# Two cross steps to one output copy, and transposes moved into the middle of the self steps, in a decoder layer's attention

## The chip, the cores and the metric

The kernel runs on one core of a Trainium2 chip. The metric is the device time of one execution in microseconds (us), as the median of several runs. TensorE (PE) does the matrix products and writes them to eight banks of PSUM; VectorE (DVE) and ScalarE (ACT) read the banks; GpSimd (POOL) works in SBUF alone; PEld is TensorE's weight load.

## The reference, cut to what matters

For eight batches of 512 tokens with 256 features the reference does a first attention, then a second attention of 16 heads of 16 features, over the 512 tokens themselves (causal) and over a context of 1024 tokens, then a routed feed-forward part, each followed by a layer norm. The change touches the second attention alone:

```python
o_self  = softmax(causal(q_s @ k_s.T * scale)) @ v_s     # 16 heads, 512 x 512
o_cross = softmax(q_c @ k_c.T * scale) @ v_c             # 16 heads, 512 x 1024
x = layernorm(x + (o_self + o_cross) @ Wp + bp)
```

Everything in it is in fp32.

## The kernel before, in words

The 16 heads are four groups of four. A group's four heads lie in four row groups of 32 rows of TensorE, and four products of one step run side by side. The loop over `s` in `batch` has 48 steps: 16 self steps (four key tiles for each of four groups, of 512, 384, 256 and 128 query columns) and 32 cross steps (eight key tiles for each group, always 512 columns). A step makes three kinds of products.

- `scores(m, r)` makes the scores of a query tile by keys. VectorE takes the maximum of each row (`maxima`, L1131 for self, L1134 for cross). These run ahead: while step `s` is worked on, the maxima of `m = s + 7` and later are taken. There are four of them (r = 0 to 3) in a cross step, and four or eight in a self step (steps 3, 7, 11 and 15 have eight).
- `scoresT(s, g)` makes the same scores transposed (L1669 for self, L1672 for cross). ScalarE takes their exponential into `work` (`probabilities`, L751), four in a step.
- `pv_part(p)` multiplies the exponentials by the values (`weighted_values`, L1681) into one bank. ScalarE copies the bank to `featA` or `featB` (`part_out`, L759), and GpSimd adds it to `featA` (`add_part`, L607). Up to step 35 one such part stands for every step; from step 36 on the products of four steps gather in one bank without such copies.

Two further products are transposes: `max_rows` turns a group's maxima (L1635), which VectorE then adds to the queries (`put_rows`, L1160) before that group's first step; `o_transpose` turns a group's outputs (L1719), which VectorE then divides by the sums (`finish`, L1168, L1170 and for cross L1174).

An fp32 product runs through TensorE in two passes, and each pass is a row of the trace. The four row groups are filled by `scores` and `scoresT` in turn, so a step of 512 columns shows as four waves of four matmuls, first the two passes of r = 0, 1 and g = 0, 1, then those of r = 2, 3 and g = 2, 3. `weighted_values` fills four column groups instead, in two waves.

Who may write a bank is settled by two rings, both walked in an order written down beforehand. Banks 0 to 3 are VectorE's ring: the scores for the maxima, the transposed rows and outputs take them in turn (`slot_uses`), and `free_slot` makes TensorE wait until VectorE is done with the use four places before. Banks 4 to 7 are ScalarE's ring: the four transposed scores of a step and its part take them in turn (`exp_slot_uses`), and `free_exp_slot` makes TensorE wait for ScalarE in the same way. From step 37 on the banks are shared out differently. TensorE takes its instructions strictly in the order in which they are written, so a product whose bank isn't free holds up all behind it.

```python
def free_exp_slot(use):
    if use >= EXP_RING:
        what, n = exp_order[use - EXP_RING]
        if what == "exp":
            pe.wait_ge(pT_ready, b * ALL_SCORES + n + 1)
        else:
            pe.wait_ge(part_copied, b * PARTS + n + 1)
```

Of the kernel before, what the change touches and what calls it, by code (L numbers as in the profile page):

```python
# [37 lines left out]
def decoder_layer(nc, x, xT, ctxT, conv_w, pe_w, qkT, vT, outT, Wk, bk, Wq, bq, Wv, bv, Wck, bck, Wcq, bcq,  # L38
# [40 lines left out]
    RING, EXP_RING = 4, 4  # L79
    BURST = 4  # L80
    BURSTS = STEPS // BURST
    PART = 1
    CHUNKS = 16
    EXTRAS = NT + 2
    EXTRA_BANKS = (7, 6, 0, 5, 7, 1)
# [16 lines left out]
    PARTS = EARLY_STEPS // PART  # L102
# [16 lines left out]
    with ctx:  # L119
# [182 lines left out]
        def spare_row(i):  # L302

            return HD * (1 - i % 2)
# [26 lines left out]

        def parts_behind(s):

            ends = [(p, PART * (p + 1) - 1) for p in range(PARTS)]
            return [p for p, e in ends if s == e + (2 if e < SELF_STEPS else 1)]

        def opens_rows(p):

            return part_of(PART * p)[2] == 0

        def adds_before(p):

# [3 lines left out]

        def part_columns(p):

            kind, _, u = part_of(PART * p)
            return slice(P * u if kind == SELF else 0, S)  # L350

        def o_rows(kind, i):
# [2 lines left out]

        def part_rows(p):

            kind, i, _ = part_of(PART * p)
            return (o_rows(kind, i) if opens_rows(p) else featB[:, adds_before(p) % 2, :])[:, part_columns(p)]

        def last_part(kind, i):

            return (first_step(kind, i) + (NT if kind == SELF else NC)) // PART - 1

        def outputs_ready(s):

# [3 lines left out]
        def slot_uses(ffn):  # L370

            order = []

            def take_maxima(first, end):
                for m in range(first, end):
                    order.extend(("max", m, g) for g in range(GH))

            for m in range(LEAD):
                if m == NT + 2:
                    order.append(("rows", SELF, 0))  # L380
                take_maxima(m, m + 1)
                if ffn and m == EXPERT_LEAD:
                    order.append(("expert",))
            for s in range(ALL_STEPS):
                if s == LATE_STEP:
                    late = len(order)
                take_maxima(maxima_before(s), maxima_before(s + 1))
                order.extend(("pv", j) for j in outputs_ready(s) if j >= SINGLES_FROM)
                order.extend(("rows",) + part for part in rows_behind(s))
                order.extend(("o",) + part for part in outputs_behind(s))  # L390
# [121 lines left out]
        def _(pool):  # L512
# [75 lines left out]
            def batch(b, prev=True, ahead=2):  # L588
# [9 lines left out]
                def add_part(p):  # L598

                    pool.wait_ge(part_copied, b * PARTS + p + 1)  # L600
                    own_wait(nc.gpsimd)
                    if adds_before(p):
                        pool.wait_ge(part_added, b * ADDS + adds_before(p))
                        own_wait(nc.gpsimd)
                    kind, i, _ = part_of(PART * p)
# [39 lines left out]
        def _(act):  # L645
# [37 lines left out]
            def batch(b, prev=True, ahead=True):  # L683
# [152 lines left out]
        def _(dve):  # L836
# [206 lines left out]
            def batch(b, prev=True, ahead=2):  # L1043
# [76 lines left out]

                def maxima(m):

                    kind, i, u = part_of(m)
                    for r in range(GH):
                        use, g = uses["max", m, r], (r + 2) % GH
                        dve.wait_ge(slot_in, base + use + 1)
                        scores = slot(uses, use)
                        if kind == SELF:
                            n = P * (u + 1)
                            own_wait(nc.vector)  # L1130
                            nc.vector.tensor_tensor_reduce(masked[:, g, 0:n], scores[:, 0:n], mask_w[:, S - n:S], -1.0, -MASKED, ALU.add, ALU.min,  # L1131
                                                           top_s[:, i % 2, u, GW * g + spare_row(i):GW * g + spare_row(i) + 1]).then_inc(slot_out, 1)
                        else:
                            nc.vector.tensor_reduce(top_half[:, i % 2, g, u // 2, u % 2:u % 2 + 1], scores, AX.X, ALU.max,  # L1134
                                                    negate=True).then_inc(slot_out, 1)
                    if kind == CROSS and u == NC - 1:
# [51 lines left out]
                for s in range(ALL_STEPS):  # L1188
# [10 lines left out]
                    for m in range(maxima_before(s), maxima_before(s + 1)):  # L1199
                        maxima(m)  # L1200
# [3 lines left out]
                    for part in rows_behind(s):  # L1204
# [3 lines left out]
                    for part in outputs_behind(s):  # L1208
                        finish(*part)
                if ahead:  # L1210
                    scores1(b + 1, 0)
# [89 lines left out]
        def _(pe):  # L1301
# [113 lines left out]
            def batch(b, prev=True, ahead=True):  # L1415
# [333 lines left out]
                for s in range(ALL_STEPS):  # L1749
                    first, n = maxima_before(s), maxima_before(s + 1) - maxima_before(s)  # L1750
                    for g in range(GH):
                        for r in range(n * g, n * (g + 1)):
                            scores(first + r // GH, r % GH)
                        scoresT(s, g)
                        if g == GH - 1 and s - SINGLES_BEHIND >= BURST * SINGLES_FROM:
# [3 lines left out]
                    for part in rows_behind(s):  # L1759
                        max_rows(*part)  # L1760
                    for part in outputs_behind(s):
                        o_transpose(*part)
                pv_step(ALL_STEPS - 2)
                if ahead:
# [84 lines left out]
```

## Time and profile before

| what | value |
|---|---|
| median of 3 runs | 2258.28 us (2256.73 to 2265.44) |
| the profiled execution's own time | 2258.12 us |
| its span, first to last instruction | 2256.4 us |
| mean granted TensorE clock | 0.964 of full speed |
| busy share PE, DVE, ACT, POOL | 94%, 81%, 66%, 23% |
| the 16 self steps of batch 2 (697.3 to 753.7 us) | 56.4 us |
| its cross steps 16 to 35 (753.7 to 816.4 us) | 62.7 us |
| its cross steps 36 to 47 (816.4 to 844.7 us) | 28.3 us |

The span holds eight batches, one after the other, each with a first attention and projections and then the 48 steps. A step is told by the start of its first exponential on ScalarE; batch 2 is taken as the example throughout. Busy time on PE covers waits inside a pipelined row of matmuls, so that it is the starts of the waves that tell the pace.

### The profile page before, as it was taken

How to read it: one execution, taken by the hardware profiler on the slowest of the kernel's cores; microseconds unless marked ns; L12 is line 12 of the kernel's file. 1: busy time of each engine (PE TensorE's matmuls, PEld its weight loads, DVE VectorE, ACT ScalarE, POOL GpSimd, SP SyncE). 2: the span in 40 equal slices, each digit the busy share in tenths (PEclk: the TensorE clock that was granted, in tenths of full speed). 3: DMA queues.
4: the chain of work that ended last, by engine and by line, in shares of the span. 5: the costliest groups of instructions: out<-in, count | busy, mean ns of one | idle time of the engine just before them, and what ended most of it. 6: DMA issues, size and time to landing. Idle time of an engine off the chain costs nothing.

```text
span 2256.4 us, 39042 instructions
## 1 busy us (share of the span) xinstructions
PE 2129.1 (94%) x13092; PEld 930.7 (41%) x13138; DVE 1835.3 (81%) x5029; ACT 1495.0 (66%) x3265; POOL 519.1 (23%) x641
## 2 busy tenths in 40 slices
PE   5999999999999999999999999999999999989983
PEld 2344334543345434444335433454334543345332
DVE  6857869689887889778897888968888788978864
ACT  2935887458864688457894588745886468845761
POOL 3012330133211350123401233013321132002310
PEclk7899999999999999999999999999999999999995
DMA  3700025000430006100170002500043000510000
GB/s 109 136 10 1 1 58 92 11 1 1 94 66 10 2 12 120 29 11 1 29 131 10 1 1 63 97 10 1 1 85 66 11 1 11 111 30 2 1 10 10
DMA packets 250857, 81.79 MB, mean 36 GB/s; under 512 B 236065, under 2 KB 247329, under 8 KB 250657
## 3 DMA queue, kind: packets, MB, share of 16 engines
q1 hardware_dynamic: 250656, 79.29, 17.3%
q8 instruction: 105, 1.72, 0.3%
q14 instruction: 96, 0.78, 0.1%
HBM read 16.35 MB, written 4.19 MB: 9 GB/s over the span
## 4 chain that ended last, share of the span: by engine, by line
PE 72%; DVE 14%; ACT 9%; issue 4%; DMA 1%; SPq 0%; POOL 0%; DVEq 0%; POOLq 0%; ACTq 0%
PE bank L1622 15%; PE bank L1681 13%; PE bank L1672 9%; PE bank L1308 6%; ACT work L692 6%; PE bank L1618 5%; PE bank L1669 4%; PE bank L1575 4%; DVE work L871 3%; PE bank L1438 3%; PE bank L1425 2%; PE bank L1461 2%; DVE top_half L1134 2%; PE bank L1635 1%; PE bank L1719 1%
## 5 line engine op out<-in xcount | busy, mean ns | idle before, releaser
L751 ACT ACTIVATE work<-bank 128x512 f32<-128x512 f32 (+3 forms) x1536 | 725.3, 550 | 329.9 <-PE bank L1669 203.0
L1134 DVE TENSOR_REDUCE top_half<-bank 128x1 f32<-128x512 f32 x1024 | 633.7, 681 | 84.4 <-PE bank L1622 83.5
L1622 PE MATMUL bank<-k_c,q_c 32*128 32x512 f32 x2048 | 559.9, 630 | 0.0
L1672 PE MATMUL bank<-q_c,k_c 32*128 32x512 f32 x2048 | 463.3, 627 | 3.9 <-DVE top_half L1134 3.9
L692 ACT ACTIVATE work<-work,neg 128x512 bf16<-128x512 bf16 x512 | 362.6, 715 | 30.5 <-DVE work L871 29.8
L1681 PE MATMUL bank<-work,v_flat 128*32 128x512 f32 (+3 forms) x3072 | 368.9, 556 | 3.1 <-DVE featA L1153 1.8
L871 DVE TENSOR_SCALAR_CACHE_REDUCE work<-bank 128x512 bf16<-128x512 f32 x512 | 322.2, 685 | 41.1 <-PE bank L1407 31.6
L607 POOL TENSOR_TENSOR featA<-featA,featB 128x512 f32<-128x512 f32 (+3 forms) x232 | 241.9, 1043 | 374.2 <-ACT featB L759 374.1
L1131 DVE CUSTOM_DVE_ANT_0 masked<-bank,mask_w 128x384 bf16<-128x384 f32 (+3 forms) x512 | 225.3, 488 | 100.3 <-PE bank L1618 96.1
L1622 PEld LDWEIGHTS bank<-k_c,q_c 32*128 32x128 f32 x2048 | 228.8, 186 | 163.5 <-DVE top_half L1134 113.5
L1669 PE MATMUL bank<-q_s,k_s 32*128 32x512 f32 (+3 forms) x1024 | 240.0, 477 | 0.0
L1672 PEld LDWEIGHTS bank<-q_c,k_c 32*128 32x128 f32 x2048 | 179.5, 184 | 107.6 <-ACT work L751 66.9
L595 POOL TENSOR_SCALAR_AFFINE_SELECT work<-work 128x512 f32<-128x512 f32 x128 | 81.2, 635 | 549.6 <-ACT work L751 549.6
L1618 PE MATMUL bank<-k_s,q_s 32*128 32x384 f32 (+3 forms) x1024 | 194.7, 474 | 4.6 <-DVE top_s L1131 4.4
L568 POOL TENSOR_SCALAR ln_var<-mv 128x4 f32<-128x4 f32 x32 | 8.8, 275 | 752.5 <-DVE mv L880 752.5
L1681 PEld LDWEIGHTS bank<-work,v_flat 128*32 128x32 f32 x3072 | 62.1, 108 | 280.6 <-ACT work L751 267.6
L1425 PE MATMUL bank<-k,q 32*128 32x512 bf16 x448 | 139.8, 389 | 16.4 <-DVE work L871 14.5
L1669 PEld LDWEIGHTS bank<-q_s,k_s 32*128 32x128 f32 x1024 | 136.5, 188 | 35.1 <-issue 25.1
L759 ACT COPY featB<-bank 128x512 f32<-128x512 f32 (+3 forms) x232 | 121.2, 522 | 24.7 <-PE bank L1681 24.6
L1438 PE MATMUL bank<-work,v 128*32 128x512 bf16 x512 | 134.6, 389 | 0.9 <-DMA work<-work 0.8
L1618 PEld LDWEIGHTS bank<-k_s,q_s 32*128 32x128 f32 x1024 | 97.7, 186 | 78.9 <-DVE top_s L1131 35.1
L1064 DVE TENSOR_SCALAR work<-work,rden 128x512 bf16<-128x512 bf16 x424 | 123.0, 349 | 4.5
(200 smaller groups left out, 2434.3 us busy)
## 6 DMA issues: line engine op xcount, KB each, us to landing
xT_pad<-xT SPq DMA_DIRECT2D x16, 256.0 KB, 2.9
ctx_sb<-ctxT SPq DMA_DIRECT2D x8, 512.0 KB, 3.4
x_res<-x SPq DMA_DIRECT2D x8, 512.0 KB, 5.0
out<-r_sb SPq DMA_DIRECT2D x8, 512.0 KB, 2.9
work<-work SPq DMA_TRANSPOSE x112, 4.4
qk_sb<-qkT SPq DMA_DIRECT2D x1, 512.0 KB, 5.1
pe_sb<-pe_w SPq DMA_DIRECT2D x1, 256.0 KB, 4.1
v_sb<-vT SPq DMA_DIRECT2D x1, 256.0 KB, 5.7
```

The source lines that it names most:

```text
L607: nc.gpsimd.tensor_tensor(rows, rows, part_rows(p), ALU.add).then_inc(part_added, 1)
L692: nc.scalar.activation(e1[:, h % E1_SLOTS, t, :], s1[:, h % 2, t, :], ACT.Exp, bias=neg1[:, h % 2, t:t + 1], scale=-1.0, accum_out=den1[:, ...
L751: nc.scalar.activation(pT[:, s % PT_SLOTS, g, q0:S], exp_bank(n)[:, 0:S - q0], ACT.Exp, scale=SCALE).then_inc(pT_ready, 1)
L871: nc.vector.tensor_scalar(s1[:, h % 2, t, :], bank[:, (NT * h + t) % A1_BANKS, :], -SCALE, None, ALU.mult, ALU.min, accum_out=neg1[:, h % ...
L1131: nc.vector.tensor_tensor_reduce(masked[:, g, 0:n], scores[:, 0:n], mask_w[:, S - n:S], -1.0, -MASKED, ALU.add, ALU.min, top_s[:, i % 2, u ...
L1134: nc.vector.tensor_reduce(top_half[:, i % 2, g, u // 2, u % 2:u % 2 + 1], scores, AX.X, ALU.max, negate=True).then_inc(slot_out, 1)
L1438: last = mm(bank[GW * g:GW * (g + 1), PV1_BANKS[h // 8], :], v1[:, h, j, :], p1T[:, h % E1_SLOTS, :, j, :], start=(h % 2 == 0 and j == 0), ...
L1618: mm(dst[:, 0:n], q_s[rows, i, P * u:n], k_s[rows, i, 0:n], start=True, stop=True, tile_position=(GW * g, 0)).then_inc(slot_in, 1)
L1622: mm(dst, q_c[rows, i, P * t:P * (t + 1)], k_c[rows, i, S * half:S * (half + 1)], start=True, stop=True, tile_position=(GW * g, 0)).then_i ...
L1669: mm(dst[:, 0:S - q0], k_s[rows, i, q0:q0 + P], q_s[rows, i, q0:S], start=True, stop=True, tile_position=(GW * g, 0)).then_inc(sT_mm, 1)
L1672: mm(dst, k_c[rows, i, P * u:P * (u + 1)], q_c[rows, i, :], start=True, stop=True, tile_position=(GW * g, 0)).then_inc(sT_mm, 1)
L1681: last = mm(dst[GW * g:GW * (g + 1), q0:S], v_flat[:, at:at + GW], pT[:, s % PT_SLOTS, g, q0:S], start=start, stop=stop, tile_position=(0, ...
```

## The change

The list `PART_STEPS` takes the place of the constant `PART = 1`. The 16 self steps keep one part each; cross steps 16 to 35 make one part for two steps, ten parts where there were twenty. Such a part multiplies the exponentials of two steps by their values into one bank, behind the step that follows the second of the two (step 18, 20, ... 36), and ScalarE copies and GpSimd adds it once. A batch has 26 parts where it had 36.

Second, in the self steps the transposes of the next group's rows (steps 2, 6, 10) and of a group's outputs (steps 7, 11, 15) no longer stand behind the step's products. They stand between its second and third quarter, on TensorE between `scoresT` of g = 1 and g = 2, on VectorE between the two halves of the step's maxima, and in VectorE's ring at that place. The rows of the first cross group (step 14) and all transposes of cross steps stay where they were.

```diff
-    PART = 1
+    PART_STEPS = [range(s, s + 1) for s in range(SELF_STEPS)] + [range(s, s + 2) for s in range(SELF_STEPS, EARLY_STEPS, 2)]
+    PARTS = len(PART_STEPS)
...
-            ends = [(p, PART * (p + 1) - 1) for p in range(PARTS)]
+            ends = [(p, steps[-1]) for p, steps in enumerate(PART_STEPS)]
             return [p for p, e in ends if s == e + (2 if e < SELF_STEPS else 1)]
+        def part_with(s):
+            return next(p for p, steps in enumerate(PART_STEPS) if s in steps)
...
+        def middle_rows(s):
+            return [part for part in rows_behind(s) if s < SELF_STEPS and part != (CROSS, 0)]
+        def middle_outputs(s):
+            return outputs_behind(s) if s < SELF_STEPS else []
+        def maxima_tiles(s):
+            tiles = [(m, r) for m in range(maxima_before(s), maxima_before(s + 1)) for r in range(GH)]
+            return tiles[:len(tiles) // 2], tiles[len(tiles) // 2:]
...
-                take_maxima(maxima_before(s), maxima_before(s + 1))
+                ahead_tiles, behind_tiles = maxima_tiles(s)
+                order.extend(("max",) + tile for tile in ahead_tiles)
+                order.extend(("rows",) + part for part in middle_rows(s))
+                order.extend(("o",) + part for part in middle_outputs(s))
+                order.extend(("max",) + tile for tile in behind_tiles)
...
-                            act.wait_ge(part_mm, b * PARTS + (s - PT_SLOTS) // PART + 1)
+                            act.wait_ge(part_mm, b * PARTS + part_with(s - PT_SLOTS) + 1)
...
-                    first, end = PART * p, PART * (p + 1)
+                    first, end = PART_STEPS[p][0], PART_STEPS[p][-1] + 1
                     free_exp_slot(exp_uses["part", p])
...
                         scoresT(s, g)
+                        if g == GH // 2 - 1:
+                            for part in middle_rows(s):
+                                max_rows(*part)
+                            for part in middle_outputs(s):
+                                o_transpose(*part)
```

On TensorE, cross steps 24 to 26 stand so before the change: each is eight products (scores L1622 and transposed scores L1672 in turn), and the values of the step before (L1681, four heads) follow it. The rows are the end of step 24 and the start of step 25.

```order
305 L1622 MATMUL bank<-k_c,q_c 128x512
306 L1672 MATMUL bank<-q_c,k_c 128x512
307 L1681 MATMUL bank<-work,v_flat 32x512 x4
308 L1622 MATMUL bank<-k_c,q_c 128x512
309 L1672 MATMUL bank<-q_c,k_c 128x512
```

After the change the same place reads so (scores L1662, transposed scores L1712, values L1721): the end of step 24, the values of steps 22 and 23, and the eight products of step 25, behind which step 26 begins at once.

```order
301 L1662 MATMUL bank<-k_c,q_c 128x512
302 L1712 MATMUL bank<-q_c,k_c 128x512
303 L1721 MATMUL bank<-work,v_flat 32x512 x8
304 L1662 MATMUL bank<-k_c,q_c 128x512
305 L1712 MATMUL bank<-q_c,k_c 128x512
```

Four value products in each gap between two steps have become eight in every other gap, and none in the gaps between.

On ScalarE the copies of the parts (L759 before, L788 now) stand between the exponentials (L751 before, L780 now); before the change, these are the copies of steps 25, 26 and 27, with the exponentials of steps 27 and 28 between them.

```order
107 L759 COPY featB<-bank 128x512
108 L751 ACTIVATE work<-bank 128x512 x4
109 L759 COPY featB<-bank 128x512
110 L751 ACTIVATE work<-bank 128x512 x4
111 L759 COPY featB<-bank 128x512
```

In the changed kernel these are the copies of steps 24 with 25, 26 with 27, and 28 with 29.

```order
98 L788 COPY featA<-bank 128x512
99 L780 ACTIVATE work<-bank 128x512 x8
100 L788 COPY featB<-bank 128x512
101 L780 ACTIVATE work<-bank 128x512 x8
102 L788 COPY featB<-bank 128x512
```

Eight exponentials stand between two copies where four stood.

The third place is self step 10 on TensorE, with the transposes of the last self group's rows. Before the change, from the third quarter of the step to the start of the next:

```order
171 L1669 MATMUL bank<-q_s,k_s 128x256
172 L1622 MATMUL bank<-k_c,q_c 128x512
173 L1669 MATMUL bank<-q_s,k_s 128x256
174 L1681 MATMUL bank<-work,v_flat 32x512 x4
175 L1635 MATMUL bank<-ident,top_s 128x128 x4
176 L1622 MATMUL bank<-k_c,q_c 128x512 x2
```

And after it:

```order
169 L1709 MATMUL bank<-q_s,k_s 128x256
170 L1675 MATMUL bank<-ident,top_s 128x128 x4
171 L1662 MATMUL bank<-k_c,q_c 128x512
172 L1709 MATMUL bank<-q_s,k_s 128x256
173 L1662 MATMUL bank<-k_c,q_c 128x512
174 L1709 MATMUL bank<-q_s,k_s 128x256
175 L1721 MATMUL bank<-work,v_flat 32x512 x4
176 L1662 MATMUL bank<-k_c,q_c 128x512 x2
```

The four transposes have moved from behind the values to ahead of the second half of the step's products.

## Rows read from the trace of the kernel before

**Rows 1.** The page, its first two parts: busy engines, and the granted clock.

```profile
PE 2129.1 (94%) x13092; PEld 930.7 (41%) x13138; DVE 1835.3 (81%) x5029; ACT 1495.0 (66%) x3265; POOL 519.1 (23%) x641
...
PEclk7899999999999999999999999999999999999995
```

**Rows 2.** The page's chain of work that ended last, by engine.

```profile
PE 72%; DVE 14%; ACT 9%; issue 4%; DMA 1%; SPq 0%; POOL 0%; DVEq 0%; POOLq 0%; ACTq 0%
```

**Rows 3.** Windows of batch 2: length, busy PE, PEld, DVE, ACT, POOL, clock.

```profile
697.30:753.70 56.40, 56.26 (x433) 28.54 (x431) 48.29 (x126) 29.80 (x79) 17.42 (x26) 1.00 0.02 8
753.70:816.40 62.70, 62.70 (x512) 24.30 (x508) 54.76 (x92) 51.13 (x102) 21.00 (x19) 1.00 0.00 1
```

**Rows 4.** Groups by line, cross steps 16 to 35: busy, mean ns | idle before, releaser.

```profile
L1134 DVE TENSOR_REDUCE top_half<-bank 128x1 f32<-128x512 f32 x80 | 49.6, 682 | 8.0 <-PE bank L1622 8.0
L751 ACT ACTIVATE work<-bank 128x512 f32<-128x512 f32 x81 | 42.0, 603 | 12.1 <-PE bank L1672 12.1
...
L1622 PEld LDWEIGHTS bank<-k_c,q_c 32*128 32x128 f32 x160 | 17.1, 183 | 14.7 <-DVE top_half L1134 11.1 <-issue 2.5
```

**Rows 5.** Timeline of PE, cross steps 25 and 26: start us, us, instruction.

```profile
780.23 0.69 PE L1622 MATMUL bank<-k_c,q_c 32*128 32x512 f32 x1
...
781.62 0.59 PE L1672 MATMUL bank<-q_c,k_c 32*128 32x512 f32 x1
...
782.16 1.06 PE L1681 MATMUL bank<-work,v_flat 128*32 128x512 f32 x8
783.15 0.69 PE L1622 MATMUL bank<-k_c,q_c 32*128 32x512 f32 x1
...
783.68 0.59 PE L1622 MATMUL bank<-k_c,q_c 32*128 32x512 f32 x1
...
784.12 0.59 PE L1622 MATMUL bank<-k_c,q_c 32*128 32x512 f32 x1
...
785.13 1.07 PE L1681 MATMUL bank<-work,v_flat 128*32 128x512 f32 x8
786.13 0.69 PE L1622 MATMUL bank<-k_c,q_c 32*128 32x512 f32 x1
```

**Rows 6.** Timeline of DVE, cross steps 25 and 26.

```profile
781.38 2.48 DVE L1134 TENSOR_REDUCE top_half<-bank 128x1 f32<-128x512 f32 x4 [0.49 <-PE bank L1622]
784.31 2.48 DVE L1134 TENSOR_REDUCE top_half<-bank 128x1 f32<-128x512 f32 x4 [0.45 <-PE bank L1622]
```

**Rows 7.** Timeline of ACT, the same steps.

```profile
784.41 2.06 ACT L751 ACTIVATE work<-bank 128x512 f32<-128x512 f32 x4 [0.38 <-PE bank L1672]
786.34 0.62 ACT L759 COPY featB<-bank 128x512 f32<-128x512 f32 x1
```

**Rows 8.** Timeline of DVE, self steps 10 and 11.

```profile
731.44 0.69 DVE L1160 TENSOR_TENSOR q_s<-bank,q_s 128x512 f32<-128x512 f32 x1 [0.20 <-PE bank L1635]
732.49 4.87 DVE L1134 TENSOR_REDUCE top_half<-bank 128x1 f32<-128x512 f32 x8 [0.36 <-PE bank L1622]
737.56 0.26 DVE L1168 RECIPROCAL rec<-bank 128x16 f32<-128x16 f32 x1 [0.20 <-PE bank L1719]
```

**Rows 9.** Timeline of PE, end of self step 10 and start of step 11.

```profile
729.75 1.07 PE L1681 MATMUL bank<-work,v_flat 128*32 128x512 f32 x8
730.75 0.66 PE L1635 MATMUL bank<-ident,top_s 128*128 128x128 f32 x4
731.33 0.70 PE L1622 MATMUL bank<-k_c,q_c 32*128 32x512 f32 x2
```

**Rows 10.** Timeline of PEld at 732.1 us, behind the rows' addition.

```profile
732.18 0.29 PEld L1622 LDWEIGHTS bank<-k_c,q_c 32*128 32x128 f32 x2 [0.32 <-DVE q_s L1160]
```

**Rows 11.** Windows: self step 7 at either clock, batch 2 and batch 3.

```profile
717.70:723.80 6.10, 6.10 (x40) 2.98 (x42) 5.54 (x15) 1.63 (x6) 1.58 (x2) 1.00 0.00 1
985.10:993.90 8.80, 8.80 (x40) 3.69 (x41) 5.74 (x16) 1.83 (x6) 1.63 (x2) 0.65 0.01 2
```

More of the change, by code:

```diff
@@ L347, in part_columns @@
         def part_columns(p):
-            kind, _, u = part_of(PART * p)
+            kind, _, u = part_of(PART_STEPS[p][0])
             return slice(P * u if kind == SELF else 0, S)
@@ L356, in part_rows, with end_rows, end_outputs @@
         def part_rows(p):
-            kind, i, _ = part_of(PART * p)
+            kind, i, _ = part_of(PART_STEPS[p][0])
             return (o_rows(kind, i) if opens_rows(p) else featB[:, adds_before(p) % 2, :])[:, part_columns(p)]
         def last_part(kind, i):
-            return (first_step(kind, i) + (NT if kind == SELF else NC)) // PART - 1
+            return part_with(first_step(kind, i) + (NT if kind == SELF else NC) - 1)
+        def middle_rows(s):
+            return [part for part in rows_behind(s) if s < SELF_STEPS and part != (CROSS, 0)]
+        def end_rows(s):
+            return [part for part in rows_behind(s) if part not in middle_rows(s)]
+        def middle_outputs(s):
+            return outputs_behind(s) if s < SELF_STEPS else []
+        def end_outputs(s):
+            return outputs_behind(s) if s >= SELF_STEPS else []
+        def maxima_tiles(s):
+            tiles = [(m, r) for m in range(maxima_before(s), maxima_before(s + 1)) for r in range(GH)]
+            return tiles[:len(tiles) // 2], tiles[len(tiles) // 2:]
         def outputs_ready(s):
@@ L386, in slot_uses @@
                     late = len(order)
-                take_maxima(maxima_before(s), maxima_before(s + 1))
+                ahead_tiles, behind_tiles = maxima_tiles(s)
[3 more added lines that the diff above has]
+                order.extend(("max",) + tile for tile in behind_tiles)
                 order.extend(("pv", j) for j in outputs_ready(s) if j >= SINGLES_FROM)
-                order.extend(("rows",) + part for part in rows_behind(s))
-                order.extend(("o",) + part for part in outputs_behind(s))
+                order.extend(("rows",) + part for part in end_rows(s))
+                order.extend(("o",) + part for part in end_outputs(s))
             order += [("pv", ALL_STEPS // BURST - 1), ("o", CROSS, HG - 1)]
@@ L604, in add_part @@
                         own_wait(nc.gpsimd)
[L605 removed]
+                    kind, i, _ = part_of(PART_STEPS[p][0])
                     rows = o_rows(kind, i)[:, part_columns(p)]
@@ L1121, in maxima, with maximum @@
                 def maxima(m):
+                    for r in range(GH):
+                        maximum(m, r)
+                def maximum(m, r):
                     kind, i, u = part_of(m)
[L1124 to L1136, printed above, removed]
+                    use, g = uses["max", m, r], (r + 2) % GH
+                    dve.wait_ge(slot_in, base + use + 1)
+                    scores = slot(uses, use)
+                    if kind == SELF:
+                        n = P * (u + 1)
+                        own_wait(nc.vector)
+                        nc.vector.tensor_tensor_reduce(masked[:, g, 0:n], scores[:, 0:n], mask_w[:, S - n:S], -1.0, -MASKED, ALU.add, ALU.min,
+                                                       top_s[:, i % 2, u, GW * g + spare_row(i):GW * g + spare_row(i) + 1]).then_inc(slot_out, 1)
+                    else:
+                        nc.vector.tensor_reduce(top_half[:, i % 2, g, u // 2, u % 2:u % 2 + 1], scores, AX.X, ALU.max,
+                                                negate=True).then_inc(slot_out, 1)
+                    if kind == CROSS and u == NC - 1 and r == GH - 1:
                         dve.wait_ge(slot_out, base + uses["max", m, GH - 1] + 1)
@@ L1198, in batch @@
                         first_qk(b + 1, *QK_LATE[s])
-                    for m in range(maxima_before(s), maxima_before(s + 1)):
-                        maxima(m)
+                    ahead_tiles, behind_tiles = maxima_tiles(s)
+                    for tile in ahead_tiles:
+                        maximum(*tile)
+                    for part in middle_rows(s):
+                        put_rows(*part)
+                    for part in middle_outputs(s):
+                        finish(*part)
+                    for tile in behind_tiles:
+                        maximum(*tile)
                     for j in outputs_ready(s):
@@ L1203, in batch @@
                             outputs(j)
-                    for part in rows_behind(s):
+                    for part in end_rows(s):
                         put_rows(*part)
@@ L1207, in batch @@
                         do(nc.vector.tensor_tensor(x_res[:], x_res[:], over_tiles(bp_row), ALU.add))
-                    for part in outputs_behind(s):
+                    for part in end_outputs(s):
                         finish(*part)
@@ L1754, in batch @@
                         scoresT(s, g)
+                        if g == GH // 2 - 1:
+                            for part in middle_rows(s):
+                                max_rows(*part)
+                            for part in middle_outputs(s):
+                                o_transpose(*part)
                         if g == GH - 1 and s - SINGLES_BEHIND >= BURST * SINGLES_FROM:
@@ L1758, in batch @@
                         pv_part(p)
-                    for part in rows_behind(s):
+                    for part in end_rows(s):
                         max_rows(*part)
-                    for part in outputs_behind(s):
+                    for part in end_outputs(s):
                         o_transpose(*part)
```

3 lines of the change are left out of this document (1 added, 2 removed).

## The prediction

> **What bounds the kernel now.** I read the page first. TensorE is busy for 94% of the span, at a clock of nearly full speed in all but the first and the last slices [rows 1], and the chain that ended last lies on it for 72% [rows 2]. That says where to look, not what limits, so I went to the windows of one batch. The cross steps 16 to 35, which the change pairs, take 62.7 us for 20 steps, with TensorE counted busy throughout, VectorE for 54.76 us and ScalarE for 51.13 us [rows 3]. VectorE's maxima sat idle 8.0 us for TensorE, 0.4 us a step, and ScalarE's exponentials 12.1 us, 0.6 us a step [rows 4]. Both wait for TensorE, by little.
>
> The timeline shows how a step is made. Step 25 starts at 780.23, step 26 at 783.15, step 27 at 786.13, so 2.92 and 2.98 us [rows 5]. A step is four waves of scores and two of values. A wave that follows one of its own kind comes 0.44 us later (783.68 to 784.12; 0.43 is taken below) [rows 5]. Six of them are 2.58 us. The rest is the price of going from scores to values and back: 0.54 instead of 0.43 us from the last wave of scores to the values (781.62 to 782.16), 1.00 instead of 0.86 us from the values to the next scores (785.13 to 786.13), and 0.53 instead of 0.43 us from the first wave of scores to the second (783.15 to 783.68) [rows 5]. Together 0.35 us, and 2.58 + 0.35 = 2.93 us is the step. TensorE's own work sets the pace here. But both other engines are close behind it, each tied to it by a ring of four banks, and the question is whether TensorE may run faster for half a step pair.
>
> **The paired parts: what they remove.** A batch has ten round trips to the values where it had twenty, so 0.35 us less of TensorE in each pair. ScalarE loses one copy in a pair, and GpSimd one addition; a copy is 0.62 us long, and holds the queue for 0.48 us (the pace of the exponentials, (2.06 - 0.62) / 3) [rows 7]. ScalarE is idle 0.38 us before each step's exponentials [rows 7], so this is worth nothing, and GpSimd is waited for only by output transposes, several steps later. The number of value products is the same.
>
> **What they add.** Step 25 now has no values behind it, and step 26 follows at once. Take the first wave of step 25 as time zero.
> - VectorE starts the first maximum 1.16 us later (784.31 less 783.15) and makes the four in 2.48 us [rows 5, 6]. The fourth ends at 3.64 us. It is paced at (2.48 - 0.68) / 3 = 0.60 us a maximum; in self step 11 eight in a row hold the same pace, 4.87 us [rows 8].
> - Step 26 needs the banks of step 25's scores, each in turn. TensorE has its own four waves of step 25 behind it at 0.53 + 3 x 0.43 = 1.82 us, but the bank of r = 3 comes back only at 3.64 us. Its weight load starts 0.05 us behind that (an addition that ended at 731.44 + 0.69 = 732.13 let a load start at 732.18) [rows 8, 10]. So the last pair of products of step 26 starts at 3.69 us. Without a wait its wave would have been the third, at 1.82 + 0.86 = 2.68 us. This is a stall of 1.01 us, spread over the step.
> - A product that starts alone needs 0.53 us to its second pass, and the values follow 0.54 us behind that [rows 5]: 3.69 + 0.53 + 0.54 = 4.76 us.
> - The values of one step with the way back are 1.00 us, and the second step's add two waves, 0.86 us [rows 5]. They share a bank, which the trace doesn't show for this kind of part; the bounds are 0.86 and 1.00 us, and I take the former, since no change of kind lies between them. Step 27 starts at 6.62 us.
>
> Before, the same two steps took 2.92 + 2.98 = 5.90 us. Each pair costs 0.72 us more. VectorE then stands idle through the long block of values: 8 x 0.60 = 4.8 us of work in 6.62 us. The ring of four banks can't lend TensorE's time from one step to the next.
>
> ScalarE's ring asks for less. The fourth exponential ends 784.41 + 2.06 = 786.47, 3.32 us behind its step's start [rows 5, 7], ahead of VectorE's 3.64. The copy ends 0.83 us behind the next step's start (786.34 + 0.62 less 786.13) [rows 5, 7] and is wanted by that step's third wave, at 0.96 us; its distance from the values is about what it was, so I take nothing, 0.1 us at most.
>
> **The sum of this part.** Nine pairs (19 with 20, up to 35 with 36) at 0.72 us are 6.5 us. The first pair, 17 with 18, still has the narrow part of step 15 behind step 17, which gives VectorE some time; between 0 and 0.72 I take half, 0.35. The steps that carry transposes of rows or outputs pay for them as before. That is 6.8 us in a batch, and all eight batches have these steps: 54.7 us. Bounds for a pair are 0.60 (the last product needs no fresh start, and the banks come back 0.02 us sooner) and 0.96 (values at 1.00, the copy late by 0.1), for the first pair 0 and 0.72: 43 to 75 us.
>
> **The transposes in the middle.** Six places in a batch. Behind the values they cost TensorE 0.58 us (730.75 to 731.33) [rows 9], and VectorE was idle 0.20 and 0.36 us around the addition of step 10, and 0.20 us ahead of the outputs of step 11 [rows 8]. In the middle they split a block of scores, which then has to be entered afresh: 0.10 us for the first wave, and about 0.10 us for leaving it. At best all VectorE idles goes, 0.56 us a place; at worst 0.20 us is added. In step 10 TensorE has four waves, values and transposes in a row, and I take it as the limit: +0.15 us. In step 11 VectorE's eight maxima are the limit, 4.87 us [rows 8], and the output work stands in the same queue either way; its idle moves, and I take 0. Three places at 0.15 us in eight batches are 3.6 us; bounds are -27 and +10.
>
> **The forecast.** 2258.1 (the profiled execution's own time) + 54.7 + 3.6 = 2316.4 us; it lies within 0.2 us of the median, so 2316 us.
>
> **Rivals.**
> - *The round trips are saved and nothing waits.* TensorE is the engine that everyone waits for [rows 3, 4], which speaks for it. Ten times 0.35 us in eight batches are 28 us: 2316.4 - 54.7 - 28 = 2234 us, faster. It decides if the bank of r = 3 is back 2.6 us behind a step's start, when TensorE would ask for it; VectorE's row says 3.64 [rows 6]. Chance 0.08.
> - The Trainium skill (TensorEngine Tiling (Array Packing), Tiling Modes, Key Properties) says that a change of the tiling mode drains TensorE. The trace agrees, with 0.11 us on the way in; by that rule alone the change would be this rival. The same page (Performance Considerations, PSUM Bottleneck) warns that tiling speeds up TensorE but not the emptying of PSUM, which is the side that I put the time on.
> - *The stall is real, but smaller.* The products of step 26 start one by one as banks come back, and the four row groups may make up for some of it, or VectorE's lag carries over into the block of values. With half the price, 0.36 us a pair, it is 2258.1 + 27 + 3.6 = 2289 us. Against it: the values can't start before the last product is through. Chance 0.11.
> - *Both parts cancel.* The middle transposes give their best, -27 us, and the pairs half their price: 2258 us, no change. Chance 0.03.
> - *The half-speed stretches of the clock.* One of them turned step 7 from 6.10 into 8.80 us, at a clock of 0.65 on average [rows 11]. More idle time on TensorE may move them; some three more or fewer are 8 us either way. This widens the forecast and is no case of its own.
>
> **How the numbers follow.** The forecast has 0.78. Its lower bound, 43 us with some 10 us gained by the middle transposes, is 2291 us. The upper one, 75 and 10 us, is 2343 us, but needs all the worst at once, so its own range is 2291 to 2332 us. The smaller stall ends at 2289, the others at 2234 and 2258. What a measurement of this kernel can tell from no change is about 0.5%, 11 us. Slower has the forecast and the smaller stall, 0.88; no change 0.04; faster 0.08. The range for 8 in 10 is 2286 to 2332 us.
>
> **What would show it.** Cross steps in the new trace alternate, some 6.6 us for two instead of 5.9, and steps 16 to 36 grow by nearly 7 us a batch. VectorE's maxima come in runs of eight without a gap, then an idle of about 1.8 us. Weight loads of the scores in even steps wait for the maxima. ScalarE has 208 copies of parts. If the pairs take 5.5 to 5.9 us, the ring was no hindrance and I am wrong. If a pair takes 6.6 and the total is yet below 2290, the middle transposes were worth more than I say; the self steps of 56.4 us [rows 3] would have shrunk by 3 us.

## The result, and the profile after

The changed kernel takes 2304.76 us (median of 4 runs, 2298.62 to 2308.49) where the kernel before takes 2257.51 us. The estimated ratio is 1.019, with a 95% interval of 1.0164 to 1.0216; the two medians stand 47 us or 2.1% apart, which that interval holds. In a second session it was 2299.95 against 2260.79 us, 1.0185 (1.0157 to 1.0213), the medians 39 us apart. So it is slower by some 2%, 39 to 47 us; 2316 us, 58 us more than before, was forecast. The profiled execution took 2306.38 us, 48.3 us more than that of the kernel before.

These are the page's busy line and its chain by engine of the changed kernel.

```profile
PE 2172.7 (94%) x13092; PEld 953.0 (41%) x13138; DVE 1816.6 (79%) x5029; ACT 1473.5 (64%) x3185; POOL 419.4 (18%) x561
...
PE 78%; DVE 10%; ACT 8%; issue 3%; DMA 1%; SPq 0%; POOL 0%; DVEq 0%; POOLq 0%; ACTq 0%
```

ScalarE has 80 instructions less and GpSimd 80 (ten in each of eight batches; 208 copies of parts are left), as the change meant it, and both are busy for less. The chain is on TensorE for 78% instead of 72% [rows 2]. Neither line tells the cause. The windows do: self steps, cross steps 16 to 35 and cross steps 36 to 47 of batch 2 of the changed kernel, with the columns of [rows 3].

```profile
705.40:762.40 57.00, 55.54 (x430) 27.52 (x428) 47.83 (x126) 29.93 (x79) 16.93 (x26) 1.00 0.02 7
762.40:829.40 67.00, 67.00 (x502) 27.09 (x496) 52.36 (x91) 48.06 (x92) 9.37 (x9) 1.00 0.00 1
829.40:859.20 29.80, 29.80 (x211) 8.90 (x208) 22.72 (x51) 25.48 (x49) 19.19 (x15) 1.00 0.06 19
```

At full clock the self steps take 57.0 us for 56.4, the cross steps with pairs 67.0 for 62.7 [rows 3], and the rest 29.8 for 28.3 (its first step carries the last pair's values). That is 6.4 us a batch, 51 us in eight; the profiled executions differ by 3 us less. In each of them TensorE's clock stood at its half for 165 us in all, but not in the same steps: in self steps for 36 us before and for 27 us after.

The timeline of TensorE shows a pair, steps 25 and 26 (scores L1662, transposed scores L1712, values L1721).

```profile
791.25 0.69 PE L1662 MATMUL bank<-k_c,q_c 32*128 32x512 f32 x1
...
793.16 0.69 PE L1712 MATMUL bank<-q_c,k_c 32*128 32x512 f32 x1
...
793.75 0.69 PE L1662 MATMUL bank<-k_c,q_c 32*128 32x512 f32 x1
...
794.35 0.69 PE L1662 MATMUL bank<-k_c,q_c 32*128 32x512 f32 x1
...
794.95 0.69 PE L1662 MATMUL bank<-k_c,q_c 32*128 32x512 f32 x1
...
796.01 1.92 PE L1721 MATMUL bank<-work,v_flat 128*32 128x512 f32 x16
797.86 0.69 PE L1662 MATMUL bank<-k_c,q_c 32*128 32x512 f32 x1
```

The pair is 797.86 - 791.25 = 6.61 us, where the kernel before has 5.90. Step 25's products start together. Those of step 26 come one by one, 0.60 us apart (793.75, 794.35, 794.95), and each is a fresh start of 0.69 us. The last one begins 3.70 us behind the pair's start, the values at 4.76 us, and they take 1.85 us with the way back. VectorE and ScalarE over the same time:

```profile
792.41 4.88 DVE L1167 TENSOR_REDUCE top_half<-bank 128x1 f32<-128x512 f32 x8 [1.73 <-PE bank L1662]
799.02 1.29 DVE L1167 TENSOR_REDUCE top_half<-bank 128x1 f32<-128x512 f32 x2 [1.73 <-PE bank L1662]
```

```profile
791.44 0.59 ACT L788 COPY featB<-bank 128x512 f32<-128x512 f32 x1 [1.31 <-PE bank L1721]
792.51 4.24 ACT L780 ACTIVATE work<-bank 128x512 f32<-128x512 f32 x8 [0.48 <-PE bank L1712]
```

Eight maxima follow without a gap, then VectorE is idle for 1.73 us. And the weight load of each late product names what it waited for:

```profile
793.75 0.18 PEld L1662 LDWEIGHTS bank<-k_c,q_c 32*128 32x128 f32 x1 [0.30 <-DVE top_half L1167]
...
794.95 0.18 PEld L1662 LDWEIGHTS bank<-k_c,q_c 32*128 32x128 f32 x1 [0.30 <-DVE top_half L1167]
```

Over cross steps 16 to 35 these weight loads wait for VectorE's maxima for 16.6 us where it was 11.1, and VectorE's maxima for TensorE for 12.5 us where it was 8.0 [rows 4]; each engine now waits longer for the other.

```profile
L1167 DVE TENSOR_REDUCE top_half<-bank 128x1 f32<-128x512 f32 x80 | 49.1, 683 | 12.6 <-PE bank L1662 12.5
...
L1662 PEld LDWEIGHTS bank<-k_c,q_c 32*128 32x128 f32 x158 | 18.7, 183 | 19.5 <-DVE top_half L1167 16.6 <-issue 2.0 <-DVE y_tmp L1203 0.3
```

### The profile page after: what moved, and what is told of

Read it like the earlier page. It is cut to its first block, busy times and chain, and to the rows that moved or that the text cites. A ratio compares the mean times of both kernels' runs of the same rounds, so it can differ in the third digit from the quotient of the medians.

```text
span 2304.7 us, 38562 instructions
## 1 busy us (share of the span) xinstructions
PE 2172.7 (94%) x13092; PEld 953.0 (41%) x13138; DVE 1816.6 (79%) x5029; ACT 1473.5 (64%) x3185; POOL 419.4 (18%) x561
## 4 chain that ended last, share of the span: by engine, by line
PE 78%; DVE 10%; ACT 8%; issue 3%; DMA 1%; SPq 0%; POOL 0%; DVEq 0%; POOLq 0%; ACTq 0%
PE bank L1662 20%; PE bank L1721 14%; PE bank L1712 9%; PE bank L1348 6%; PE bank L1658 6%; ACT work L721 5%; PE bank L1709 4%; PE bank L1615 4%; DVE work L900 4%; PE bank L1478 3%; PE bank L1465 2%; PE bank L1501 2%; PE bank L1675 2%; PE bank L1759 2%; ACT k_c L754 1%
## 5 line engine op out<-in xcount | busy, mean ns | idle before, releaser
L780 ACT ACTIVATE work<-bank 128x512 f32<-128x512 f32 (+3 forms) x1536 | 735.1, 549 | 305.4 <-PE bank L1709 211.0
L1662 PE MATMUL bank<-k_c,q_c 32*128 32x512 f32 x2048 | 610.8, 633 | 0.0
L1712 PE MATMUL bank<-q_c,k_c 32*128 32x512 f32 x2048 | 520.5, 630 | 0.0
L721 ACT ACTIVATE work<-work,neg 128x512 bf16<-128x512 bf16 x512 | 362.5, 714 | 30.6 <-DVE work L900 29.8
L1721 PE MATMUL bank<-work,v_flat 128*32 128x512 f32 (+3 forms) x3072 | 353.4, 553 | 0.9 <-ACT work L780 0.7
L1662 PEld LDWEIGHTS bank<-k_c,q_c 32*128 32x128 f32 x2048 | 239.4, 185 | 217.3 <-DVE top_half L1167 169.9
L1712 PEld LDWEIGHTS bank<-q_c,k_c 32*128 32x128 f32 x2048 | 211.9, 183 | 92.4 <-ACT work L780 45.3
L636 POOL TENSOR_TENSOR featA<-featA,featB 128x512 f32<-128x512 f32 (+3 forms) x152 | 140.7, 926 | 514.5 <-ACT featB L788 514.5
L1721 PEld LDWEIGHTS bank<-work,v_flat 128*32 128x32 f32 x3072 | 69.7, 109 | 270.7 <-ACT work L780 198.2
L788 ACT COPY featB<-bank 128x512 f32<-128x512 f32 (+3 forms) x152 | 69.9, 460 | 93.4 <-PE bank L1721 93.4
```

Of the source, the lines that this page charges most:

```text
L721: nc.scalar.activation(e1[:, h % E1_SLOTS, t, :], s1[:, h % 2, t, :], ACT.Exp, bias=neg1[:, h % 2, t:t + 1], scale=-1.0, accum_out=den1[:, ...
L1662: mm(dst, q_c[rows, i, P * t:P * (t + 1)], k_c[rows, i, S * half:S * (half + 1)], start=True, stop=True, tile_position=(GW * g, 0)).then_i ...
L1712: mm(dst, k_c[rows, i, P * u:P * (u + 1)], q_c[rows, i, :], start=True, stop=True, tile_position=(GW * g, 0)).then_inc(sT_mm, 1)
L1721: last = mm(dst[GW * g:GW * (g + 1), q0:S], v_flat[:, at:at + GW], pT[:, s % PT_SLOTS, g, q0:S], start=start, stop=stop, tile_position=(0, ...
```

## The experiments

The theory: the place of the values makes the loss, by way of the rings. TensorE gets through a step without values before the banks of its scores are free, and loses more there than the saved round trip gives. The rivals: the cost lies in the values themselves or in the shared bank, or in the transposes. All runs start from the changed kernel.

**The two halves of the change by themselves.** `e1_pairs_only` puts all transposes back behind their steps:

```diff
-            return [part for part in rows_behind(s) if s < SELF_STEPS and part != (CROSS, 0)]
+            return []
...
-            return outputs_behind(s) if s < SELF_STEPS else []
+            return []
...
-            return outputs_behind(s) if s >= SELF_STEPS else []
+            return outputs_behind(s)
```

`e3` to `e6`, `e9` and `e10` carry this edit too; their diffs below leave it out, and show of some long lines only the part that changes.

> The paired parts alone, all transposes where they were before. If the pairs make the whole loss by way of VectorE's ring of four banks, a plain pair of cross steps takes 6.6 us (5.9 before), steps 16 to 47 take about 96.9 us a batch as in the changed kernel (90.9 before), and the time is 2258 + 8 x 6.0 = 2306 us, 2.1% over the kernel before. The rival, that the middle transposes make a good part of the loss (for instance by moving the half-speed stretches of the clock), expects 2285 us or less.

Measured: 2310.23 us against 2263.39 us before in the same session, 1.0192 (1.0148 to 1.0237). Steps 16 to 47 take 67.0 + 29.9 = 96.9 us in an undisturbed batch, as in the changed kernel. The pairs alone make a loss as large as that of the whole change.

`e2_middle_only` keeps the transposes in the middle and takes the pairs back:

```diff
-    PART_STEPS = [...] + [range(s, s + 2) for s in range(SELF_STEPS, EARLY_STEPS, 2)]
+    PART_STEPS = [...] + [range(s, s + 1) for s in range(SELF_STEPS, EARLY_STEPS)]
```

> The transposes in the middle of self steps alone, one part a step everywhere. The forecast priced them at 0.45 us a batch, the changed kernel's undisturbed self steps show 0.6 us (57.0 for 56.4). So the theory expects 57.0 us for the self steps of a batch at full clock, 62.7 us for cross steps 16 to 35, and 2258 + 5 = 2263 us, hardly to be told from the kernel before. The rival, that they give time back and hide a larger loss of the pairs, expects 2250 us or less.

Measured: 2244.47 us, 0.9924 (0.9898 to 0.9949), so 19 us faster than the kernel before. In the trace the self steps of batch 2 take the same 57.0 us as in the changed kernel, 0.6 us more than before, and cross steps 16 to 35 the 62.7 us of the kernel before. Both theories as put fell: at full clock the self steps got longer and the cross steps stayed, and the gain lies in the clock, as the runs on the transposes below bear out. The mean granted clock was 0.969 to 0.976 in its runs, and 0.956 to 0.968 in those of the kernel before.

**Is it the place of the values, or the shared bank?** `e3_two_parts_together` goes back to a part, a copy and an addition for each step, but puts the values of two steps behind the even one:

```diff
-[range(s, s + 2) for s in range(SELF_STEPS, EARLY_STEPS, 2)]
+[range(s, s + 1) for s in range(SELF_STEPS, EARLY_STEPS)]
...
-            return [p for p, e in ends if s == e + (2 if e < SELF_STEPS else 1)]
+            return [p for p, e in ends if s == (e + 2 if e < SELF_STEPS else e + 1 + (e + 1) % 2)]
```

> One part, one copy and one addition for every cross step as before, but the value products of two steps stand together behind each even step, as in the changed kernel; transposes as before. It takes only the place of the value products from the change, not the saved copies. If the place alone makes the stall (VectorE's ring), a plain pair takes 6.6 to 6.75 us and the total is 2306 to 2315 us. If the way in which two steps share a bank or a copy is the cost, a pair goes back to 5.9 us or less and the total is 2258 us or less.

Measured: 2311.89 us in one run. ScalarE's timeline shows both copies, and a pair of 804.26 - 797.65 = 6.61 us:

```profile
797.65 4.24 ACT L780 ACTIVATE work<-bank 128x512 f32<-128x512 f32 x8 [0.48 <-PE bank L1712]
802.27 0.59 ACT L788 COPY featA<-bank 128x512 f32<-128x512 f32 x1 [0.39 <-PE bank L1721]
803.19 0.59 ACT L788 COPY featB<-bank 128x512 f32<-128x512 f32 x1 [0.33 <-PE bank L1721]
804.26 1.09 ACT L780 ACTIVATE work<-bank 128x512 f32<-128x512 f32 x2 [0.48 <-PE bank L1712]
```

Two copies and two additions, and the pair is as long as in the changed kernel, to a hundredth of a microsecond. So the place of the values makes the loss, and the copy and the addition that the change saves are worth nothing here.

**Does the price follow VectorE's pace?** `e4_quads` gathers four steps in a part:

```diff
-[range(s, s + 2) for s in range(SELF_STEPS, EARLY_STEPS, 2)]
+[range(s, s + 4) for s in range(SELF_STEPS, EARLY_STEPS, 4)]
```

> Cross steps 16 to 35 in parts of four steps, five in a batch, transposes as before. The ring theory gives four steps as follows: the fourth maximum of the first step ends 3.64 us behind its start, each further step without values adds VectorE's four maxima, 2.40 us, so the last products of the fourth step start at 3.69 + 4.80 = 8.49 us, the values at 9.56 us, and they take 1.00 + 3 x 0.86 = 3.58 us: 13.1 us for four steps, where two pairs take 13.2 and four single steps 11.8. Total about 2258 + 8 x 5 x 1.3 = 2310 us, within 10 us of the pairs. The rival by round trips saved expects each quad to be 3 x 0.35 us shorter than four single steps, 10.8 us, and 2215 us in all; a price that grows with the length of the block of values (0.7 us for every step added to it) expects 13.9 us and 2342 us.

Measured: 2320.32 us in one run, 10 us above what was expected, at a clock of 0.959 (0.957 to 0.969 in the runs with pairs alone). Steps 25 to 28 of batch 2 on ScalarE:

```profile
801.39 6.63 ACT L780 ACTIVATE work<-bank 128x512 f32<-128x512 f32 x12 [0.48 <-PE bank L1712]
809.13 2.06 ACT L780 ACTIVATE work<-bank 128x512 f32<-128x512 f32 x4 [1.11 <-PE bank L1712]
814.00 0.59 ACT L788 COPY featA<-bank 128x512 f32<-128x512 f32 x1 [2.81 <-PE bank L1721]
815.13 1.09 ACT L780 ACTIVATE work<-bank 128x512 f32<-128x512 f32 x2 [0.54 <-PE bank L1712]
```

They take 815.13 - 801.39 = 13.74 us. Step 27 carries four transposes of a group's outputs, taken at the 0.58 us of the four in [rows 9]; without them it is 13.16 us, and 13.1 was expected. A quad costs what two pairs cost, since each further step without values goes at VectorE's 2.4 us.

**Both rings faster.** If waiting for the banks is the cause, the sign of the pairs must turn when the banks come back in time. `e5_half_single` and `e6_half_pairs` take the maxima and exponentials of cross steps over half the columns, the first with one step a part, the second with pairs. The other half of that work is left out; TensorE's is whole:

```diff
-scores, AX.X, ALU.max,
+scores[:, 0:S // 2], AX.X, ALU.max,
...
-                    q0 = P * s % S if s < SELF_STEPS else 0
+                    q0 = P * s % S if s < SELF_STEPS else S // 2
```

> A control for the next run. One part a step and transposes as before, but in cross steps VectorE takes its maximum over 256 of 512 columns and ScalarE its exponential of 256 of 512 columns; the rest of the work is left out, TensorE's is complete. TensorE's own waves pace the kernel before, so both theories expect that cross steps hardly change: 2.93 us a step, 5.86 a pair, where some steps took 2.98.

Measured: 2203.43 us. A step is 2.92 us; the pair from step 25 to 27 is 766.43 - 760.58 = 5.85 us. The total is 54 us lower than before because other steps did wait for VectorE or ScalarE. At full clock the self steps take 53.0 us for 56.4 (from step 7 on they take maxima of cross scores too), steps 16 to 35 take 61.2 for 62.7, half of that in step 29, and the steps from 36 to the start of 47 24.9 for 26.3.

```profile
760.58 1.46 ACT L780 ACTIVATE work<-bank 128x256 f32<-128x256 f32 x4 [0.48 <-PE bank L1712]
...
763.50 1.46 ACT L780 ACTIVATE work<-bank 128x256 f32<-128x256 f32 x4 [0.54 <-PE bank L1712]
...
766.43 0.66 ACT L780 ACTIVATE work<-bank 128x256 f32<-128x256 f32 x2 [0.48 <-PE bank L1712]
```

> The same halved maxima and exponentials with the parts in pairs; what is left out is the same as in the control. The ring theory says that the stall needs VectorE's 0.60 us a maximum. Halved, the last maximum of the first step ends at about 2.8 us instead of 3.64, and TensorE wants its bank at 2.68: a stall of about 0.15 us is left, against 0.35 us saved on the round trip. So a pair should now be SHORTER than two single steps: 5.65 us for 5.86, and this kernel about 8 x 10 x 0.2 = 16 us faster than its control. If the cost lay in the values themselves (two steps into one bank, eight products in a row), the pair would stay 0.7 us longer than the control's, 56 us slower.

Measured: 2195.38 us, 8 us or 0.4% below the control (ratios to the kernel before 0.972, 0.9693 to 0.9747, and 0.9758, 0.9733 to 0.9784; the intervals overlap). The trace is clearer: the pair is 771.44 - 765.70 = 5.74 us.

```profile
765.70 1.46 ACT L780 ACTIVATE work<-bank 128x256 f32<-128x256 f32 x4 [0.48 <-PE bank L1712]
767.41 1.46 ACT L780 ACTIVATE work<-bank 128x256 f32<-128x256 f32 x4 [0.25 <-PE bank L1712]
...
771.44 0.66 ACT L780 ACTIVATE work<-bank 128x256 f32<-128x256 f32 x2 [0.54 <-PE bank L1712]
```

With the banks back nearly in time, the same pairing saves 0.1 us a pair instead of costing 0.7. The value products are those of the changed kernel, so the cost isn't in them. The saving is half of the 0.2 us expected, and the first pair and the steps behind the last one give back 0.2 us each in a batch. What is left is 0.4 us a batch, 3.4 us in all, so that the trace, not the total, shows the sign turned.

**Which ring.** `e9_halfmax_pairs` halves the maxima alone, `e10_halfexp_pairs` the exponentials alone, with pairs kept. The first edit is `e9`'s, the second `e10`'s:

```diff
-scores, AX.X, ALU.max,
+scores[:, 0:S // 2], AX.X, ALU.max,
```

```diff
-                    q0 = P * s % S if s < SELF_STEPS else 0
+                    q0 = P * s % S if s < SELF_STEPS else S // 2
```

> Pairs, transposes as before, and VectorE's maxima of cross steps over 256 of 512 columns (the other half of that work is left out); ScalarE's exponentials whole. Which ring holds TensorE next? ScalarE's fourth exponential ends 3.32 us behind a step's start, where VectorE's fourth maximum ended at 3.64, so the ring theory expects a pair of 6.62 - 0.29 = 6.3 us: ScalarE's ring takes over at once. If VectorE alone were the cause, a pair would fall to 5.7 us as with both halved.

> Pairs, transposes as before, and ScalarE's exponentials of cross steps over 256 of 512 columns (the other half is left out); VectorE's maxima whole. The ring theory has VectorE's ring as the later one, so a pair stays at 6.6 us. If ScalarE's ring held TensorE, it would fall by 0.3 us or more.

Measured: 2243.5 and 2297.88 us in one run each; the first is below the kernel before, since its self steps gain too, as in `e5_half_single`. With halved maxima VectorE's runs start at 778.56 and 784.84, a pair of 6.28 us; with halved exponentials ScalarE's groups start at 793.62 and 800.24, 6.62 us.

```profile
778.56 2.47 DVE L1167 TENSOR_REDUCE top_half<-bank 128x1 f32<-128x256 f32 x6 [2.60 <-PE bank L1662]
...
784.84 0.42 DVE L1167 TENSOR_REDUCE top_half<-bank 128x1 f32<-128x256 f32 x1 [2.60 <-PE bank L1662]
```

Both came as expected. VectorE's ring holds TensorE in a pair. With the maxima halved the pair falls by 0.33 us only, and to 5.74 us when the exponentials are halved too: ScalarE's ring comes next.

**The transposes and the clock.** `e7_middle_rows` and `e8_middle_outputs` are `e2_middle_only` with only the rows, or only the outputs, in the middle. The first has `middle_outputs` empty and `end_outputs` whole, the second `middle_rows` empty:

```diff
-            return outputs_behind(s) if s < SELF_STEPS else []
+            return []
...
-            return outputs_behind(s) if s >= SELF_STEPS else []
+            return outputs_behind(s)
```

```diff
-            return [part for part in rows_behind(s) if s < SELF_STEPS and part != (CROSS, 0)]
+            return []
```

> Only the transposes of rows (steps 2, 6 and 10) in the middle of their step, all else as before. The self steps at full clock should show plus 0.5 us a batch (step 2 shorter by 0.2, steps 6 and 10 longer by 0.5 and 0.2). By the count of waves 2258 + 4 us. The theory that the middle transposes win by fewer half-speed stretches of TensorE's clock expects, if the rows are what matters, a mean granted clock of 0.97 or more and 2245 us; if the outputs matter, a clock of 0.96 and 2262 us.

> Only the transposes of outputs (steps 7, 11 and 15) in the middle of their step, all else as before. By the count of waves plus 0.1 us a batch, 2259 us. With the clock theory, if the outputs matter (the half-speed stretches of the kernel before fall on step 7 in every second batch), a mean granted clock of 0.97 or more and 2240 us; if not, a clock of 0.96 and 2259 us.

Measured: rows 2259.66 us, 1.0015 (0.9989 to 1.0041), clock 0.956 to 0.970; outputs 2244.24 us, 0.9944 (0.9925 to 0.9962), clock 0.972 to 0.973, with the kernel before at 2257.54 us and 0.962 to 0.968. The rows alone gain nothing; the outputs alone gain 13 us, where both together gained 19 in another session, with intervals that overlap. So the outputs' place gives most of the gain, if not all. No step at full clock got shorter by it: this window is the self steps of batch 2, 56.5 us for 56.4.

```profile
690.80:747.30 56.50, 56.36 (x434) 28.76 (x431) 48.01 (x128) 29.77 (x79) 16.80 (x26) 1.00 0.02 8
```

**Both halves together.** In the last session the changed kernel ran again, with nothing edited, beside pairs with only the outputs in the middle:

```diff
-            return [part for part in rows_behind(s) if s < SELF_STEPS and part != (CROSS, 0)]
+            return []
```

> The changed kernel itself, timed beside the kernel before in one session with the next run, since the middle transposes gave 13 to 19 us alone and the changed kernel shows little of that. If the gain by the clock is kept, it is 10 us or more below pairs alone (which stood at a ratio of 1.019 to the kernel before), so 1.013 or less, at a granted clock of 0.97. If it is lost beside the pairs, the ratio is 1.019 or more, at 0.965.

> Pairs, and only the outputs' transposes in the middle (steps 7, 11, 15), the rows' behind their step. By the count of waves 0.5 us a batch less than the changed kernel, since the rows in the middle cost steps 6 and 10 something. If outputs in the middle keep the clock up beside pairs as they do without them, clock 0.97 and 2290 us; if the pairs undo that, clock 0.965 and 2302 us.

Measured: 2299.95 us at 1.0185 (1.0157 to 1.0213), clock 0.963 to 0.971; and 2292.94 us at 1.0142 (1.012 to 1.0165), clock 0.969 to 0.973. The second is what was expected of outputs that keep the clock up. For the changed kernel the case of a lost gain fits better, but its interval overlaps that of pairs alone, and so does that of `e12_pairs_middle_outputs`, so how much of the clock each keeps is open. The profiled executions lean the same way: their self steps stood at half the clock for 27 and 24 us in the two of the changed kernel and for 7 us with the outputs alone in the middle. With pairs alone it was 22 us, in an execution 15 us below that kernel's median.

The fastest with all its work are the two with single steps and the outputs in the middle, 2244 us.

## Why the prediction was right

The mechanism came as written, and so did its signs: pairs of 6.6 us, eight maxima without a gap and then 1.73 us of idle, loads that wait for the maxima. The forecast was 12 us too high against the first median and 16 us against the second. Against the profiled execution, 2306.4 us, it was 10 us too high: the pairs were put 8 us too high and the transposes 1 us too low, and the clock, put at nothing, took off some 3 to 4 us.

- *TensorE paces the plain cross steps.* Shown by `e5_half_single`: with half the work on both other engines such a step is still 2.92 us. It doesn't hold for all: step 29 took 3.68 us before, and 2.93 us there.
- *The stall at the bank of r = 3.* The last products were put at 3.69 us behind the pair's start, the values at 4.76, the next pair at 6.62. The trace has 3.70, 4.76 and 6.61. The second step's values add 1.85 - 1.00 = 0.85 us, 0.86 was taken.
- *The saved copy and addition are worth nothing.* Shown by `e3_two_parts_together`.
- *The sum of the pairs was too large*: 6.8 us a batch forecast, 5.9 measured (67.0 + 29.8 against 62.7 + 28.3 gives 5.8, the starts of the exponentials 5.9), so 47 us in eight batches where 54.7 was taken. The term "nine pairs at 0.72 us" is the one mis-sized. Eight of them cost 0.70 to 0.79 us, but the pair 29 and 30 costs nothing: step 29 already took 3.68 us before, 0.7 more than its neighbours, so the two steps took 7.19 us, and take 7.20 now; the 0.7 us was a wait for VectorE or ScalarE, for it is gone in `e5_half_single`. I read one clean pair and multiplied it. The first pair cost 0.22 us, 0.35 was taken.
- *The transposes in the middle.* For the outputs nothing was taken, and 0.04 us a place came. For the rows 0.15 us a place was taken; step 2 fell by 0.2, steps 6 and 7 together rose by 0.5, steps 10 and 11 by 0.25. With the rows alone in the middle (`e7_middle_rows`) undisturbed self steps took 56.86 us for 56.35, 0.17 a place. The sum of 3.6 us in the forecast stands against some 5 us at full clock.
- *The clock was named as worth 8 us either way.* In the changed kernel's profiled execution it stayed within that, 3 to 4 us. With single steps it was worth more: the outputs' place alone made 13 us by it. It was left out of the sum, since I saw no reason for a direction, and these runs show one. That little of it came beside the pairs was luck for the forecast, since nothing in the working says so.
- *The rival of saved round trips* failed for the reason given: banks are back at 3.64, not at 2.6 us. `e6_half_pairs` shows that it would have won otherwise. The Trainium skill (TensorEngine Tiling (Array Packing), Tiling Modes, Key Properties) says that changing the tiling mode drains TensorE. The traces of both kernels agree, with 0.54 and 0.53 us (795.48 to 796.01) from the last wave of scores to the values instead of 0.43. That section gives no price for the change of mode, and says nothing of who waits when changes of mode are made rarer. The smaller stall and the two parts that cancel didn't come.
- *A slip in the chances.* The forecast and the smaller stall are 0.78 + 0.11 = 0.89, and the parts that cancel 0.03; 0.88 and 0.04 were written. The forecast doesn't hang on it.

## What to carry to other kernels

A ring of few banks ties two engines step by step, and averages don't help: TensorE with some 5.5 us of work and VectorE with 4.8 us for two steps needed 6.6, because one ran ahead in the first and the other starved in the second. Before gathering work into larger and rarer blocks, follow one bank round the ring through the step that is left without the block: when it is filled, when the reader ends, when the writer asks for it. And multiply a clean step's price only by the steps that are as clean.

## What the runs showed of the hardware that was not expected

Where a few transposes stand changes how often TensorE's clock is halved. In the kernel before, the granted clock falls to its half (1.2 of 2.4 GHz) for 6.8 us in the middle of self step 7 of batch 3, 2.4 us ahead of the output transposes (990.12 us); the windows are cut at the fall and at the step's end.

```profile
985.10:987.70 2.60, 2.60 (x14) 1.55 (x13) 2.60 (x10) 0.55 (x2) 0.00 (x0) 1.00 0.00 0
987.70:993.90 6.20, 6.20 (x28) 2.14 (x28) 3.14 (x8) 1.28 (x4) 1.63 (x2) 0.50 0.01 3
```

The step takes 8.8 us then instead of 6.1 [rows 11]. When the clock fell, TensorE was at work on the step's scores, and two of their weight loads had waited 0.26 and 0.32 us for VectorE. The stretch reaches into step 8, and the self steps of batch 3 take 59.6 us where those of batch 2 take 56.4: 3.2 us lost for 6.8 us at half speed, so by estimate some 5 us for each 10.

With the outputs' transposes in the middle of their steps, most of these stretches are gone. The self steps of all eight batches stood at half the clock for 36 us before, for 34 us with the rows alone in the middle, for 10 us with the outputs alone, and for none with both (all with single cross steps). Over the whole profiled executions it was 165, 162, 125 and 111 us. The 26 us that the outputs took away are worth some 12 us by that estimate, and 13 us were measured. These are one profiled execution each, but the clocks and times of all runs go the same way. Why the transposes' place does this was not tried, and stays open.
